# Second cross attention of a decoder kernel: value projections moved from the opening into the first five steps

## The reference, cut to what matters

```python
q = ln @ Wq
kv_input = jnp.concatenate([xn, ln], axis=-2)
kv = kv_input @ Wkv
k, v = jnp.split(kv, 2, axis=-1)
q, k, v = (heads(q), heads(k), heads(v))      # 8 heads of 64
sim = jnp.einsum('bhid,bhjd->bhij', q, k)
attn = jax.nn.softmax(sim, axis=-1)
out = jnp.einsum('bhij,bhjd->bhid', attn, v)
return out @ Wout
```

## Time and profile before

| what | value |
|---|---|
| median of 3 runs (lowest to highest) | 2134.19 us (2133.84 to 2134.27) |
| profiled execution: time | 2132.76 us |
| profiled execution: span | 2131.0 us |
| TensorE busy | 85% of the span |
| VectorE busy | 51% |
| ScalarE busy | 40% |
| GpSimd busy | 24% |
| mean granted TensorE clock | 0.898 of full |

### The profile page before, as it was taken

The page is one execution under the profiler, slowest core; times in us unless marked ns, Lnnn a source line. Parts: engine busy times, 40 slices in busy tenths (PEclk is TensorE's granted clock), DMA queues, the critical chain, the costliest instruction groups (busy, mean ns, idle before and its releaser), DMA issues.

```text
span 2131.0 us, 27189 instructions
## 1 busy us (share of the span) xinstructions
PE 1814.4 (85%) x10505; PEld 1033.6 (49%) x10505; DVE 1087.0 (51%) x2162; ACT 850.8 (40%) x1406; POOL 516.0 (24%) x574
## 2 busy tenths in 40 slices
PE   4598898877997988979888988798988978979888
PEld 3354654633354555543445564434554643455546
DVE  5576476553654553346455534562645255636442
ACT  2222222213643453336343533463534425625342
POOL 2476276200350021005300300071003001700120
PEclk7799899987998989989999898899998988989899
DMA  7000000000000000000000000000000000000000
GB/s 199 1 1 0 0 0 0 0 0 0 1 1 0 1 1 1 6 0 1 1 1 1 1 1 6 0 1 1 1 1 1 1 6 0 1 1 1 1 1 6
DMA packets 18260, 13.27 MB, mean 6 GB/s; under 512 B 7643, under 2 KB 14783, under 8 KB 18143
## 3 DMA queue, kind: packets, MB, share of 16 engines
q1 hardware_dynamic: 17951, 11.65, 1.9%
q10 hardware_dynamic: 192, 0.02, 0.0%
HBM read 10.55 MB, written 1.05 MB: 5 GB/s over the span
## 4 chain that ended last, share of the span: by engine, by line
PE 66%; issue 10%; DVE 7%; ACT 6%; POOL 5%; POOLq 5%; DVEq 1%; DMA 0%; SPq 0%; ACTq 0%
PE PSUM L1255 6%; PE PSUM L1432 5%; PE PSUM L1424 5%; PE PSUM L422 4%; PE PSUM L1332 4%; PE PSUM L1303 4%; PE PSUM L378 3%; PE PSUM L1319 2%; POOLq L863 2%; PE PSUM L1397 2%; POOLq L861 2%; POOL OTA L865 2%; POOL OTA L860 2%; PE PSUM L400 2%; PE PSUM L1315 2%
## 5 line engine op out<-in xcount | busy, mean ns | idle before, releaser
L577 DVE TENSOR_REDUCE negmax<-PSUM 128x2 f32<-128x1024 f32 (+3 forms) x256 | 256.5, 1016 | 138.6 <-PE PSUM L384 81.8
L233 POOL TENSOR_TENSOR rstd<-var,neg_half 128x4 f32<-128x4 f32 (+1 forms) x33 | 33.5, 1015 | 973.9 <-DVE var L223 888.5
L559 ACT ACTIVATE PTA<-PSUM 128x1024 f32<-128x1024 f32 (+1 forms) x224 | 214.3, 963 | 107.3 <-PE PSUM L422 106.3
L1255 PE MATMUL PSUM<-PTA,VA 128*64 128x512 f32 x512 | 146.5, 650 | 4.7 <-ACT OTA L538 2.2
L1687 ACT ACTIVATE PTA<-PSUM,V 128x512 f32<-128x512 f32 x128 | 88.0, 687 | 136.1 <-PE PSUM L1424 133.1
L639 POOL TENSOR_TENSOR QXA<-QXA,PTA 128x1024 f32<-128x1024 f32 x56 | 132.7, 2370 | 35.2 <-ACT PTA L559 31.8
L422 PE MATMUL PSUM<-QSTACK,KSTACK 64*128 64x512 f32 (+3 forms) x512 | 116.0, 473 | 22.3 <-ACT PTA L559 9.0
L2019 DVE TENSOR_REDUCE nmax<-PSUM 128x1 f32<-128x589 f32 x128 | 97.7, 766 | 65.0 <-PE PSUM L1309 65.0
L1424 PE MATMUL PSUM<-YT,W 128*128 128x512 f32 x256 | 127.1, 646 | 0.0
L1432 PEld LDWEIGHTS PSUM<-W,PTA 128*128 128x128 f32 x1024 | 118.2, 192 | 10.0 <-issue 9.9
L1432 PE MATMUL PSUM<-W,PTA 128*128 128x128 f32 x1024 | 119.7, 275 | 0.0
(11 more groups left out here) (415 smaller groups left out, 3709.6 us busy)
## 6 DMA issues: line engine op xcount, KB each, us to landing
W<-in_L_ffn_W_dram SPq DMA_DIRECT2D x1, 2048.0 KB
out_dram<-X SPq DMA_DIRECT2D x4, 256.0 KB, 2.3
PTA<-in_L_attn_Wc_dram SPq DMA_DIRECT2D x1, 640.0 KB
PTA<-in_L_attn_Wo_dram SPq DMA_DIRECT2D x1, 512.0 KB
Wkv<-in_L_xattn_Wkv_dram SPq DMA_DIRECT2D x1, 512.0 KB
KMA<-in_L_attn_ttt_proj_dram SPq DMA_DIRECT2D x1, 256.0 KB
QXA<-in_L_ffn_w_up_dram SPq DMA_DIRECT2D x1, 256.0 KB
QXA<-in_L_ffn_w_down_dram SPq DMA_DIRECT2D x1, 256.0 KB
```

The source lines that it names most:

```text
L559: A.activation(probs, PSUM[:, at:at + 2, 0:probs.shape[2]], ACT.Exp).then_inc(m_exp, 1)
L577: last = Vv.tensor_reduce(negmax[:, s % 2, t, :], PSUM[:, k:k + 2, at:at + a.width(t)], AX.X, ALU.max, negate=True)
L1255: last = T.matmul(PSUM[e * VD:(e + 1) * VD, 6, :], V1[:, c, h * VD:(h + 1) * VD], full.probsT(s, c)[:, e, :], start=(c == 0), stop=(c == Q ...
```

## The change

The five value projections leave the opening. `project_values(c)` issues the c-th of them in step c of the first five, behind `turn(2c-1)` and ahead of `turn(2c)`, and all five go through bank 7. The first waits for the fourth copy of keys (which leaves bank 7), each later one for the copy of the values before it. ScalarE copies projection j at the end of step j, behind the exponential of unit 2j+1. The scores of step 0 now wait themselves for the four query copies and two key copies, and the first value product for all five value copies. The number and size of the instructions stay as they were.

```diff
--- before.py
+++ after.py
@@ -1282,22 +1282,22 @@
                     T.matmul(bank(kb), Wkv1[:, p * P:(p + 1) * P], YT[:, :], start=True, stop=True)
                     T.matmul(bank(kb + 1, CTX), Wkv1[:, p * P:(p + 1) * P], CN[:, :], start=True, stop=True)\
                         .then_inc(s_e_k, 1)
-                for c in range(5):
-                    if c < 4:
-                        pe.wait_ge(s_e_qs, b * 4 + c + 1)
-                        T.matmul(bank(c), YT[:, c * P:(c + 1) * P], Wkv1[:, 512:1024], start=True, stop=True)\
-                            .then_inc(s_e_v, 1)
+                def project_values(c):
+                    if c == 0:
+                        pe.wait_ge(s_e_ks, b * 4 + 4)
                     else:
-                        pe.wait_ge(s_e_ks, b * 4 + 3)
-                        T.matmul(PSUM[0:CTX, 4, :], CN[:, :], Wkv1[:, 512:1024], start=True, stop=True)\
-                            .then_inc(s_e_v, 1)
-                pe.wait_ge(s_e_ks, b * 4 + 4)
-                pe.wait_ge(s_e_vs, b * 5 + 5)
+                        pe.wait_ge(s_e_vs, b * 5 + c)
+                    rows = P if c < 4 else CTX
+                    T.matmul(PSUM[0:rows, 7, :], YT[:, c * P:(c + 1) * P] if c < 4 else CN[:, :], Wkv1[:, 512:1024],
+                             start=True, stop=True).then_inc(s_e_v, 1)
 
                 def scores(j):
                     v, t = divmod(j, QT)
                     if j:
                         pe.wait_ge(s_exp, b * UNITS + 2 * j - 1)
+                    else:
+                        pe.wait_ge(s_e_qs, b * 4 + 4)
+                        pe.wait_ge(s_e_ks, b * 4 + 2)
                     for e in range(2):
                         rows = slice(64 * e, 64 * e + 64)
                         T.matmul(bank(2 * ((2 * j + e) % 3)), QX[rows, v, t * P:(t + 1) * P], KX[rows, v, 0:SEQ],
@@ -1325,6 +1325,8 @@
                         pe.wait_ge(s_cmoved, b * UNITS + XG * (v + 1))
                         if v:
                             pe.wait_ge(s_outs, b * 3 + v)
+                        else:
+                            pe.wait_ge(s_e_vs, b * 5 + 5)
                     rows = P if c < 4 else CTX
                     for e in range(2):
                         h = 2 * v + e
@@ -1360,6 +1362,8 @@
                         scores(j)
                     if j:
                         turn(2 * j - 1)
+                    if j < 5:
+                        project_values(j)
                     for pair, c in {0: ((v - 2, 4),), 1: ((v - 1, 0),), 2: ((v - 1, 1), (v - 1, 2)), 3: ((v - 1, 3),)}[t]:
                         if pair >= 0:
                             value(pair, c)
@@ -1632,10 +1636,10 @@
                 for p in range(4):
                     act.wait_ge(s_e_q, b * 4 + p + 1)
                     A.activation(QX[:, p, :], bank(p), ACT.Copy, scale=XD ** 0.5).then_inc(s_e_qs, 1)
-                for c in range(5):
+                def copy_projected(c):
                     rows = P if c < 4 else CTX
                     act.wait_ge(s_e_v, b * 5 + c + 1)
-                    A.activation(VX[0:rows, c, :], PSUM[0:rows, c, :], ACT.Copy).then_inc(s_e_vs, 1)
+                    A.activation(VX[0:rows, c, :], PSUM[0:rows, 7, :], ACT.Copy).then_inc(s_e_vs, 1)
 
                 def exp(i):
                     act.wait_ge(s_max, b * UNITS + i + 1)
@@ -1662,6 +1666,8 @@
                     exp(2 * j)
                     move_context(2 * j)
                     exp(2 * j + 1)
+                    if j < 5:
+                        copy_projected(j)
                     if j >= 8 and j % QT == 0:
                         copy_values(j // QT - 2)
                 move_context(UNITS - 1)
```

## The result

The changed kernel took 2085.94 us (median of 4 runs, 2085.26 to 2087.07), the kernel before 2134.23 us in the same comparison: a ratio of 0.9773, 95% interval 0.9756 to 0.9790. It is 48.3 us faster; 38.7 us had been forecast, and the range held the time.

The account below looks back on a forecast made before the run. TensorE, busy 85% of the span, and its granted clock were taken as the bound. 5.27 + 3.45 + 0.95 = 9.67 us a batch, 38.7 us for four, gave a median of 2095.5 us, range 2077 to 2114.

Parts of the forecast that it names:

- The first two terms: Second cross attention: first scores start 5.27 us earlier, and the first three steps lose 3.45 us of low clock, each batch.
- The third: Stages after this one: the full clock returns sooner behind their projections, 0.95 us less a batch, bounds -0.95 and +2.85.
- The serial stretch: Stage opening: first scores follow the last keys directly, moving from 661.23 to 655.96, 5.27 us less a batch.
- The first three steps: Step 0 to the scores of step 3: the half-clock stretch goes, 14.73 us shrinking by 3.45 us a batch.
- TensorE's projections, ScalarE's copies, the waits: Early steps: moved work fits idle time, cost 0; if uncovered, projections cost 4.4 us and copies 3.0 us a batch.
- The clock in later stages: Later stages: an earlier start likely shortens the next stage's wait for full clock, 0.95 us a batch.
- rival C: Next stage: the later half-clock stretch from 769.4 to 782.9 goes as well, 4.3 us more a batch; 2078 us, chance 0.16.
- The rule on transposes: Early steps, half transposes: if transposes don't count towards the clock, low clock returns and only 5.27 us a batch is gained.
- B: First steps: the low clock stays and only the 5.27 us a batch of the opening is gained; 2113 us, chance 0.12.
- D: Steps with projections: clock falls and never returns, steps grow to 6.80 us, 6.5 us a batch slower; 2160 us, chance 0.03.
- E: Early steps: ScalarE's moved copies are not covered, costing 3.0 us a batch; 2108 us, chance 0.08.
- F: Later stages: 19 us more low clock per batch gives back 9.7 us, nothing gained in all; 2134 us, chance 0.03.

Follow-up runs that it names:

- e1: Kernel before with five extra products, read by nobody, in steps 0 to 4 where the changed kernel projects values; serial opening kept: 2120.85 us, ratio 0.9933.
- e2: Changed kernel with each projection of values behind turn(2j) instead of ahead of it: 2108.76 us, ratio 0.9881.
- e3: Changed kernel with every ScalarE copy of projected values issued twice, the first into unused columns: 2082.94 us, ratio 0.9748.
- e4: Changed kernel with each projection of values done twice on TensorE: 2107.08 us, ratio 0.9869.
- d3: Changed kernel with two extra products, read by nobody, at the end of the stage of each batch: 2107.65 us, ratio 0.9876.
- w4: Changed kernel with unread products ahead of the transposes of all five openings, six in this stage's, five ahead of the gate, four elsewhere: 2050.86 us, ratio 0.9615.
- w2: Changed kernel with four unread products ahead of the transposes of all five openings of a batch: 2067.14 us, ratio 0.9683.
- w1: Changed kernel with four unread products ahead of the transposes of two openings, this stage's and the next one's: 2080.21 us, ratio 0.9742.
- w3: Kernel before with four unread products ahead of the transposes of all five openings of a batch: 2089.04 us, ratio 0.9784.
- d4: Changed kernel with four extra products, read by nobody, at the end of the stage of each batch: 2091.48 us, ratio 0.9809.

## Why the prediction was right, point by point

The range held the time, 9.6 us below the forecast. The first two terms, 8.72 us a batch or 34.9 us, measured 33.7 us. The third was too small, which is why the time lies below this case's own range of 2088 to 2103 us.

- **The bound.** TensorE and its clock set the time, and no other engine's stretch mattered: right.
- **The serial stretch (5.27 us).** Measured 5.14, 5.09, 4.37 and 5.19 us: right to 0.2 us in three batches. In batch 2 the opening itself had 5.5 us at half clock instead of 3.9.
- **The first three steps (3.45 us).** Measured 3.47 us in all four batches, and steps of 3.75 to 3.76 us. The filling was shown to be enough with the old opening (e1); that it is needed was not (e2). The forecast idle piece came out: some 0.8 us ahead of the first turn, shown as 0.69 us.
- **TensorE's projections, ScalarE's copies, the waits (0).** Right. The slack was under-rated on both engines (e3, e4): a second copy costs nothing, a second projection 0.44 us a step.
- **The clock in later stages (0.95 us a batch).** This term was mis-sized. The next stage's first part gave 5.4, 5.6, 0.5 and 4.0 us, 3.9 us a batch; with all that lies outside this stage and that part counted in, 3.0 us a batch of span are left, just beyond the bound of 2.85 us. The step was right that the full clock would come sooner behind the projections (3.7 us instead of 5.3), and it priced the shorter wait; it left to rival C that a whole later low stretch hangs on the same arrival. C is what happened in batches 0 and 1 and mostly in 3, not in 2. C's own price, 4.3 us a batch, was near. How much of this the kernel gets is luck of arrival and no merit of the new order: with two products more (d3) the gain in the next stage's first part is gone, and two executions of e3 came 8 and 9 us below the changed kernel with no less work.
- **The rule on transposes.** The steps of the changed kernel ran at 1.00 throughout, as the settled ones of before did. The Trainium skill (TensorE: Matmul & The Clock Gate, Part 4: PE-mode transpose) says that a transpose doesn't count as busy time for the clock as a matmul does. As the prediction read it, these steps would have met the low clock as before; the same reading would hold for those of e2. Both ran at 1.00 (661.3 to 672.6, and in e2 656.9 to 741.0), so the measurement decides against that reading here; how much a transpose counts isn't shown.
- **Rivals B, D, E, F.** B (the low stretch stays) and D (it stays down) didn't occur in the profiled execution of any run of the changed order. E is excluded by e3. F needed the later stages to take the gain back; d3 shows that this can be: two products more, and 15 us of the 48 are lost to later stages.

## What to carry to other kernels

Where TensorE bounds a kernel, read each stage's granted clock beside its busy time, and price a change by both: here the shorter opening was 19.8 of 45.7 us of the gain and the clock nearly all of the rest. A time that moves by more or less than the edit can explain is to be tested with an idle shift: a few products that nobody reads, on the path, show how much of it is arrival. And pauses of TensorE that other engines cause at stage openings can be filled with such products; in w4 the last of them ended 0.55 us ahead of the work that follows, while the shorter filling of w2 ended 2.27 us ahead of it and left the fall in place. Such filling moves the arrivals behind it as well, so each is to be measured (w1).

## What the runs showed of the hardware

- The granted clock fell behind pauses as short as 1.74 us (with 0.76 us shortly before), and behind 2.27 and 0.87 us (w2); it didn't fall behind 1.75 us in e2, where no pause had stood ahead of the scores, nor behind 0.77 and 0.68 us in e1. The same two pauses of 0.77 and 1.74 us were followed by 10.2 us of half clock in the kernel before, and by 3.4 us in three batches of w3.
- Execution time is not monotonic in work: 1.74 us more a batch gave -12.6 us, 3.48 us more gave +13.4 us; in the changed kernel +21.7 and +5.5 us.
- Some kernels spread more than others from run to run: e3 from 2076.5 to 2089.0 us, d4 from 2089.7 to 2099.2, w4 from 2047.2 to 2054.1, against 1.8 us for the changed kernel. In e3 and w4 the faster runs had the higher mean clock (w4: 0.946 and 0.947 against 0.942), in d4 the slowest the lowest (0.914 against 0.917 to 0.919). That they differ by arrivals is likely but not shown, since one execution of each was profiled.
